# Counting stage of a graph network kernel: one-hots for four steps in one VectorE instruction, slots multiplied by a keep factor

## The reference

```python
msg = h[row] * norm[:, None]
out = jax.ops.segment_sum(msg, col, num_segments=n)      # graph convolution
...
agg = jax.ops.segment_sum(x[src], dst, num_segments=x.shape[0])   # GIN
h = x + agg
```

## Time and profile before

| | us |
|---|---|
| median of three runs | 7,153.08 |
| lowest and highest run | 7,152.85 and 7,164.23 |
| the profiled execution | 7,145.89 |
| its span, first to last instruction | 7,144.2 |
| counting stage in it, 3589.0 to 4665.8 | 1,076.8 |
| GpSimd busy in the stage | 1,074.5 |
| ScalarE | 899.7 |
| VectorE | 803.1 |
| TensorE | 769.0 |

### The profile page before, as it was taken

One profiled execution on the slowest core, in us unless ns is written; L12 is line 12 of the kernel. 1 busy time (PEld: TensorE's weight loads), 2 busy tenths in 40 slices (PEclk: granted clock), 3 DMA queues, 4 the chain that ended last, 5 costly groups with the idle time before them and its releaser, 6 DMA issues. The chain is left out here.

```text
span 7144.2 us, 114758 instructions
## 1 busy us (share of the span) xinstructions
PE 5082.2 (71%) x23608; PEld 3897.9 (55%) x23609; DVE 4037.3 (57%) x10176; ACT 2624.3 (37%) x5843; POOL 3151.9 (44%) x4006
## 2 busy tenths in 40 slices
PE   5666666556666645664467777769999998999986
PEld 3445454234444535553211111159989988889876
DVE  4666666343333347877577777744444455445443
ACT  1111111111111110001078888845555554445433
POOL 3777776027777730000099999921111111112111
PEclk8999988765555556665655555579999999999998
DMA  4333333025555522331112222233333343224331
GB/s 126 98 98 98 98 98 89 15 87 156 158 158 157 157 80 78 97 96 43 29 64 73 73 73 73 74 133 127 142 131 136 128 153 130 109 100 149 123 109 60
DMA packets 523425, 745.71 MB, mean 104 GB/s; under 512 B 57861, under 2 KB 419336, under 8 KB 523240
## 3 DMA queue, kind: packets, MB, share of 16 engines
q1 hardware_dynamic: 440008, 512.24, 21.2%
q0 software_dynamic: 83232, 231.06, 11.4%
HBM read 584.89 MB, written 158.20 MB: 104 GB/s over the span
## 5 line engine op out<-in xcount | busy, mean ns | idle before, releaser
L1956 PE MATMUL ps<-moving,parts 128*128 128x384 f32 (+1 forms) x11662 | 2075.0, 335 | 223.2 <-DVE moving L2162 112.4
L1956 PEld LDWEIGHTS ps<-moving,parts 128*128 128x128 f32 x11662 | 1971.9, 190 | 295.7 <-DVE moving L2162 164.2
L444 POOL DMA_INDIRECT arena<-table_kv,arena x1664 | 1646.8, 990 | 520.4 <-issue 442.9
L2019 ACT ACTIVATE moving<-counts 128x1152 fp32r<-128x1152 uint8 (+1 forms) x952 | 1060.5, 1125 | 684.6 <-PE ps L1956 675.0
L1894 POOL CAST moving<-counts 128x1152 fp32r<-128x1152 uint8 (+1 forms) x357 | 402.9, 1129 | 2034.1 <-PE ps L1956 1985.1
L2162 DVE CAST moving<-counts 128x1152 fp32r<-128x1152 uint8 (+1 forms) x714 | 812.0, 1143 | 562.6 <-PE ps L1956 554.1
L1621 PE MATMUL ps<-arena 128*128 128x392 bf16 x1568 | 769.0, 505 | 372.4 <-POOL arena L1571 278.0
L1571 POOL TENSOR_SCALAR arena<-arena 128x128 bf16<-128x128 f16 x1568 | 1018.7, 663 | 0.1
L1643 ACT ACTIVATE arena<-ps 128x392 uint8<-128x392 f32 x1568 | 824.4, 529 | 334.1 <-PE ps L1621 326.6
L1621 PEld LDWEIGHTS ps<-arena 128*128 128x128 bf16 x1568 | 163.4, 104 | 978.3 <-ACT arena L1643 774.7
L1586 DVE TENSOR_SCALAR arena<-arena 128x392 bf16<-128x392 f16 x1572 | 559.6, 356 | 192.0 <-PE ps L1621 189.9
(11 more groups left out here) (290 smaller groups left out, 5331.9 us busy)
## 6 DMA issues: line engine op xcount, KB each, us to landing
counts<-adjacency SPq DMA_DIRECT2D x105, 2352.0 KB, 8.4
adjacency<-arena SPq DMA_DIRECT2D x784, 98.0 KB, 1.7
edge_values<-arena SPq DMA_DIRECT2D x208, 256.0 KB, 3.2
arena<-edge_values SPq DMA_DIRECT2D x208, 256.0 KB, 3.1
arena<-table_kv,arena POOLq DMA_INDIRECT x1664
counts<-adjacency SPq DMA_DIRECT2D x14, 1568.0 KB, 6.6
table_kv<-arena POOLq DMA_DIRECT2D x14, 896.0 KB, 4.7
rest<-table_norm SPq DMA_DIRECT2D x60, 192.0 KB, 5.3
```

Of the source, the lines that this page charges most:

```text
L444: pool.indirect_dma_start(m.ring4[:, r * HALF + k, 0:f], None, table, bass.IndirectOffsetOnAxis(m.idx4[:, r * HALF + k:r * HALF + k + 1], ...
L1956: mm = pe.matmul(m.bank(g % 2, n * P), d.parts[SOURCE[u]][:, s + q, t_, :], moving[:, q * n * P:(q + 1) * n * P], start=(s + q == 0 and t_ ...
L2019: act.activation(to, of, ACT.Copy).then_inc(by_act, 1)
```

## The change

GpSimd has no part in the stage any more. VectorE makes both one-hots of a half, each in one two-tensor compare of 16-bit numbers: the numbers 0 to 391, each written four times in a row (`count_fours`), against the four steps' `lo` or `place` values, read again for each number. So the four steps lie next to each other in the result, and TensorE reads its operands with a step of four elements (`by_lo[:, r, :, k]`). Slots are not cleared: the add becomes one multiply-add, slot times `keep` plus counts, where `keep` is 0 on the first step of a window and 1 after it. ScalarE only evicts. The wait for the stores moves from ScalarE to VectorE, ahead of the one-hots. The table `clean` and the zeros go, `keep` comes, `lo` and `place` are 16-bit.

```diff
-        self.lo = take(WCOLS)
-        self.place = take(WCOLS)
+        self.lo = take(WCOLS, F16)
+        self.place = take(WCOLS, F16)
-        self.clean = take(WCOLS, I32)
+        self.keep = take(WCOLS)
+        self.count_fours = split(take(HALF * WIDE, F16), WIDE, HALF)
-        self.by_lo = split(take(4 * HALF * P, BF16), 4, HALF, P)
-        self.lo_now = split(take(4 * HALF), 4, HALF)
-        self.by_place = split(take(2 * HALF * WIDE, BF16), 2, HALF, WIDE)
+        self.by_lo = split(take(4 * HALF * P, BF16), 4, P, HALF)
+        self.by_place = split(take(2 * HALF * WIDE, BF16), 2, WIDE, HALF)
...
-            pool.memset(m.zeros, 0.0).then_inc(made, 1)
...
-            then(dve.tensor_copy(m.count_to, m.wramp[:, 0:WIDE]))
+            then(dve.tensor_copy(m.count_fours, copies(m.wramp[:, 0:WIDE], 2, HALF)))
...
-            for table, ahead, size in ((m.ring, 0, WIDE // 2), (m.clean, RING // 2, WIDE // 4)):
-                then(dve.tensor_scalar(table, m.window, float(ahead), None, ALU.add))
-                then(dve.tensor_scalar(table, table, RING - 1, None, ALU.bitwise_and))
-                then(dve.tensor_scalar(table, table, float(size), None, ALU.mult))
+            then(dve.tensor_copy(m.ring, m.window))
+            then(dve.tensor_scalar(m.ring, m.ring, RING - 1, None, ALU.bitwise_and))
+            then(dve.tensor_scalar(m.ring, m.ring, float(WIDE // 2), None, ALU.mult))
+            then(dve.memset(m.keep[:, 0:1], 0.0))
+            then(dve.tensor_tensor(m.keep[:, 1:WCOLS], m.window[:, 1:WCOLS], m.window[:, 0:WCOLS - 1], ALU.is_equal))
...
-        @block.gpsimd
-        def _(pool):
-            def fetch(j, r):
...
-            def half(j, r):
-                wait(pool, lo_hot, (j - 2) * HALF)
-                fetch(j + 1, (r + 1) % 4)
...
-                for k in range(HALF):
-                    pool.tensor_scalar(m.by_lo[:, r, k, :], m.count_to[:, 0:P], m.lo_now[:, r, k:k + 1], None,
-                                       ALU.is_equal).then_inc(lo_hot, 1)
...
-            def one_hot(s, h, k):
-                dve.tensor_scalar(m.by_place[:, h, k, :], m.count_to, m.place[:, ds(s, 1)], None,
-                                  ALU.is_equal).then_inc(hot, 1)
-
-            def half(j, h, at):
-
+            def one_hots(j, r):
+
+                dve.tensor_tensor(m.by_lo[:, r], m.count_fours[:, 0:P, :],
+                                  copies(m.lo[:, ds(j * HALF, HALF)], 1, P), ALU.is_equal).then_inc(lo_hot, 1)
+                dve.tensor_tensor(m.by_place[:, r % 2], m.count_fours,
+                                  copies(m.place[:, ds(j * HALF, HALF)], 1, WIDE), ALU.is_equal).then_inc(hot, 1)
+
+            def half(j, r, at, whole=None, seen=None):
+
+                h = r % 2
                 wait(dve, product, j * HALF)
+                if whole is not None:
+                    dve.wait_ge(whole, seen)
+                one_hots(j + 1, (r + 1) % 4)
                 for k in range(HALF):
                     s = j * HALF + k
-                    one_hot(s + HALF, 1 - h, k)
                     if k % 2 == 0:
                         dve.wait_ge(moved, s + 2)
-                    if k == 0:
-                        wait(dve, cleaned, (j - 1) * HALF)
                     wait(dve, added, s)
                     to = m.slot_pairs[:, ds(at[k], WIDE // 2)]
-                    dve.tensor_tensor(to, to, m.counted_pairs[:, h, k, :], ALU.add).then_inc(added, 1)
...
+                    dve.scalar_tensor_tensor(to, to, m.keep[:, ds(s, 1)], m.counted_pairs[:, h, k, :],
+                                             ALU.mult, ALU.add).then_inc(added, 1)
...
-                    pe.wait_ge(lo_hot, s + 1)
-                    pe.wait_ge(hot, s + 1)
+                    if k == 0:
+                        pe.wait_ge(lo_hot, j + 1)
+                        pe.wait_ge(hot, j + 1)
                     wait(pe, moved, s - UNROLL + 1)
-                    pe.matmul(bank(r % 2, k), m.by_lo[:, r, k, :], m.by_place[:, r % 2, k, :], start=True, stop=True).then_inc(product, 1)
+                    pe.matmul(bank(r % 2, k), m.by_lo[:, r, :, k], m.by_place[:, r % 2, :, k], start=True, stop=True).then_inc(product, 1)
...
-                    if at is not None:
-                        act.wait_ge(cleaned, s - HALF)
-                        act.activation(m.slots_as_f32[:, ds(at[k], WIDE // 4)], m.zeros,
-                                       ACT.Copy).then_inc(cleaned, 1)
...
-                if not first:
-
-                    sp.wait_ge(cleaned, (j - 2) * HALF + 1)
```

More of the change, by code:

```diff
@@ L1550, in count_edges @@
 def count_edges(nc, m, adj):
-    with Phase(nc, "ce", "hot fetched begun lo_hot product moved added cleaned stored0 stored1 stored2 stored3") as (
-            block, hot, fetched, begun, lo_hot, product, moved, added, cleaned, *stored):
+    with Phase(nc, "ce", "hot lo_hot product moved added stored0 stored1 stored2 stored3") as (
+            block, hot, lo_hot, product, moved, added, *stored):
         bank = lambda h, k: m.bank(h * HALF + k, WIDE)
-        @block.gpsimd
-        def _(pool):
-            def fetch(j, r):
-                pool.tensor_copy(m.lo_now[:, r, :], m.lo[:, ds(j * HALF, HALF)]).then_inc(fetched, 1)
-            def half(j, r):
-                wait(pool, lo_hot, (j - 2) * HALF)
-                fetch(j + 1, (r + 1) % 4)
-                pool.wait_ge(fetched, j + 1)
-                wait(pool, product, (j - 3) * HALF)
-                pool.sem_inc(begun, 1)
-                for k in range(HALF):
-                    pool.tensor_scalar(m.by_lo[:, r, k, :], m.count_to[:, 0:P], m.lo_now[:, r, k:k + 1], None,
-                                       ALU.is_equal).then_inc(lo_hot, 1)
-            fetch(0, 0)
-            for r in range(4):
-                half(r, r)
-            with pool.Fori(1, WTURNS // 2) as i:
-                for r in range(4):
-                    half(4 * i + r, r)
         @block.vector
@@ L1610, in _ @@
                 for r in range(4):
-                    half(4 * i + r, r % 2, at[r * HALF:])
+                    half(4 * i + r, r, at[r * HALF:], stored[(r + 1) % 4], 32 * (i + (r + 1) // 4))
         @block.tensor
@@ L1630, in _, with half @@
         def _(act):
-            regs = registers(nc, act, "ceact", 4 * HALF)
-            def half(j, h, at=None, whole=None, seen=None):
-                if j is not None and not (isinstance(j, int) and j < 2):
+            def half(j, h):
+                if not (isinstance(j, int) and j < 2):
                     act.wait_ge(added, (j - 1) * HALF)
-                if whole is not None:
-                    act.wait_ge(whole, seen)
                 for k in range(HALF):
-                    s = j * HALF + k
-                    act.wait_ge(product, s + 1)
+                    act.wait_ge(product, j * HALF + k + 1)
                     act.activation(m.counted[:, h, k, :], bank(h, k), ACT.Copy).then_inc(moved, 1)
-                    if at is not None:
-                        act.wait_ge(cleaned, s - HALF)
-                        act.activation(m.slots_as_f32[:, ds(at[k], WIDE // 4)], m.zeros,
-                                       ACT.Copy).then_inc(cleaned, 1)
-            act.sem_inc(cleaned, HALF)
-            half(0, 0)
-            half(1, 1)
-            at = load_steps(act, regs, m.clean, HALF, (RING - 1) * WIDE // 4)
-            half(2, 0, at)
-            half(3, 1, at[HALF:], stored[0], 32)
+            for r in range(4):
+                half(r, r % 2)
             with act.Fori(1, WTURNS // 2) as i:
-                at = load_steps(act, regs, m.clean, i * 4 * HALF - HALF, (RING - 1) * WIDE // 4)
                 for r in range(4):
-                    half(4 * i + r, r % 2, at[r * HALF:], stored[(r + 1) % 4], 32 * (i + (r + 1) // 4))
+                    half(4 * i + r, r % 2)
         @block.sync
@@ L1677, in _ @@
             for r in range(4):
-                half(r, r, True)
+                half(r, r)
             with sp.Fori(1, WTURNS // 2) as i:
```

11 lines of the change are left out of this document (4 added, 7 removed).

## The result

The changed kernel takes 7,621.9 us (median of 4 runs, 7,620.2 to 7,626.4), the kernel before on the same chip 7,155.0 (4 runs, 7,152.9 to 7,164.2). The ratio is 1.0653, 95% interval 1.0636 to 1.067: slower by 467 us. The forecast was 7,615.

The account below looks back on a forecast made before the run. GpSimd's one-hots were taken as the bound, VectorE's own program as the next. 392 halves of 3.46 us (1,356), turns (181) and filling (2) gave a 1,539 us stage, +462; 7,146 + 462 + 7 = 7,615 us, range 7,400 to 7,720.

Parts of the forecast that it names:

- One-hots in pairs: VectorE's two four-step compares handle 16-bit elements two at a time: 0.42 and 0.97 us per half.
- Rival C: VectorE's one-hots do not take pairs: 1.09 us more per half, 8,040 us in total; chance 0.08.
- The multiply-add at 0.42 us: VectorE's fused operation on 196 elements goes one element at a time: 0.36 + 0.06 us for its per-partition operand.
- Rival B: VectorE's multiply-add takes pairs: 0.32 us each, a half 3.06 us, 7,470 us in total; chance 0.15.
- rival E: VectorE's multiply-adds run without gaps and take pairs: a half 2.19 us, 7,127 us in total; chance 0.05.
- The gap between them at 0.21 us: On VectorE each multiply-add starts 0.21 us after the one it waits for ends; bounds 0.14 and 0.28.
- The turn, 1.87 us over a normal half: VectorE's register load, spreading and loop arithmetic every sixteen steps, no longer covered: 1.87 x 97 = 181 us.
- rival D: TensorE's operands with a step of four cost four cycles a column: 1.31 us per matmul, 8,125 us; chance 0.03.
- The line rule: For TensorE's operand reads, a 16-byte line must be hit at least twice; the step does this, so it is free.
- Who could be late: TensorE and ScalarE have counts ready about 2.6 us after the one-hots, hidden behind VectorE's 3.4 us or more.

## Why the prediction was right

The stage was forecast at 1,539 us and took 1,551; by its terms:

- **One-hots in pairs** (0.42 and 0.97 us): 0.420 and 0.968, where one by one would have been 0.69 and 1.79. Rival C is out. The Trainium skill, "Vector Engine (DVE) Microarchitecture Reference", section 5.1, says that a row read again and again still goes two at a time with two 16-bit sources; the trace agrees.
- **The multiply-add at 0.42 us**, one element at a time: 421 ns, and 422 in the kernel with the load in pieces. Rival B is out, and with it E. The same section leaves scalar_tensor_tensor out of the operations with a faster mode; the trace agrees, 421 ns against 259 of the plain add of the same size.
- **The gap between them at 0.21 us**: 0.18, 0.25 and 0.18, mean 0.20. That makes the half 3.43 and not 3.46, 12 us less over the stage. The rows of before from which it was taken stand in another stage, with other sizes; it carried over.
- **The turn, 1.87 us over a normal half**: 2.00, and the half behind it is longer by 0.12 besides. This is the term that was too small, by 0.25 us and 24 us over the stage. The row of before that it was taken from was a seam behind a short add of 0.25; it had 1.96 us idle, the seam of the changed kernel 1.91, but the multiply-add ahead of it is 0.17 us longer. The idle time carries over, not the time from start to start. The two errors have opposite signs and leave the stage 12 us over its forecast.
- **Reading with a step of four** (rival D): the matmul went from 505 to 525 ns and the weight load from 104 to 120, far from the 1.31 us per matmul of the rival, and hidden behind VectorE. The kernels with short one-hots in fours, where only the weights are read with a step, lie between (513 or 514 and 113), so the strided operands have a small price, and not none; that the matmuls also come four at a time in the changed kernel was not separated from it. The line rule that the prediction cites from the Trainium skill ("SBUF — State Buffer", section "Door 1: The DMA port swizzle") has it as free; the trace agrees but for these 20 and 16 ns.
- **Who could be late**: nobody. No idle time of VectorE of weight is ended by TensorE, and the 21 us that bear ScalarE's name are a gap that is as long without it. The new wait for the stores cost nothing that a row shows.

The median came closer than the stage, 7,622 against 7,615, and that is luck. The stage grew by 474.8 us and not 462, and 5.6 came outside it where nothing was expected, 18.4 us in all. But the forecast had added 7 us, by which the profiled execution of before lay under the median known then, and the profiled execution of the changed kernel lies 4.5 over its median; that takes 11.5 away again. One sum of a rival is off by little: by its own terms rival E needs a half below (1,077 - 191 - 2) / 392 = 2.26 us, not 2.27.

That VectorE's seam was hidden before and is open now was argued in the prediction; the two kernels that move and cut the load show what it costs: 61 us come back when the load stands behind the one-hots and 165 when it is also cut, and interleaving gives 114. The loss of 475 us is split by the runs in one way: 203 with the one-hots, 272 with the multiply-adds on top, of which 4 x 0.16 us x 392 = 251 are the slower operation. Taken the other way, the multiply-adds alone cost 198, and the one-hots 277 on top. Interleaving and the load in pieces were not put together; by their two gains the stage would be 1,551 - 114 - 165 = 1,272 us, an estimate, and still slower than before.

## What to carry to other kernels

Moving work from an engine that is full to one that is 75% busy needs the second one's program laid out in order of time, since its idle time may be a load, a loop's branch and waits on itself which only the old bound had covered. Before an add and a clear are fused, ask whether the fused operation keeps the faster mode of the plain one: here two instructions on two engines (262 and 322 ns side by side) became one of 421 on the engine that was short of time. And where dependent instructions stand in a row, put independent ones between them; where a register load stands at a loop's head, cut it and put each piece behind enough queued work: here 1.23 us covered a piece wholly and 0.42 us did not, and from the 0.71 to 0.74 us that it took there, some 0.75 is an estimate of what is needed.

## What the runs showed of the hardware that was not expected

- A register load costs by its numbers: 347 ns for 4, 1,100 for 16, 2,292 for 32 on VectorE's queue (medians), 63 and 75 ns for each further number ((1,100 - 347) / 12 and (2,292 - 1,100) / 16). A longer turn saves nothing of it.
- The queue goes on past an instruction that is under way: a load of 347 ns right behind 1.23 us of one-hots left no idle time, behind a one-hot of 0.42 alone it cost 0.38. The Trainium skill, "Perfetto Trace Analysis", "DVE / Act Engine Instruction", says that the sequencer is ready for the next instruction as soon as it has pushed one; the trace agrees, up to the length of what is queued.
- A VectorE instruction that waits for the one before it through a register operation starts 0.14 to 0.25 us after its end (0.29 behind the seam); with another between, it starts 0.08 or 0.09 us ahead of that one's end.
- The same load of sixteen took 1,284 ns in the kernel with the one-hots alone and 1,335 in the one with the keep factors alone (medians), 1,100 in the changed one. What lengthens it was not tried.
- VectorE's plain add takes 243 to 369 ns in the kernel before, and up to 357 to 374 in the four with GpSimd clearing; it takes 251 to 266 in the three with GpSimd idle (one-hots alone, and the two with short one-hots and ScalarE clearing). The 392-column compare goes the same way: 306 to 448 ns before, 311 to 325 in the last two. That GpSimd does it was not tried by itself.
